# Two attention and mixture-of-experts layers on one core: the routing tables, the shared chunks and the opening of the second layer are rearranged

## The reference, cut to what matters

```python
x = x + L0_attention(layernorm(x), ctx)      # x: 16 sequences of 112 rows, 256 wide; 16 heads; ctx: 375 rows
x = x + L0_ffn(layernorm(x))
x = x + L1_attention(layernorm(x), ctx)
x = x + L1_ffn(layernorm(x))
# L0_ffn: each of the 1792 rows goes to 8 of 64 experts (inner width 128),
#   chosen by sigmoid scores in groups, and to one shared expert (inner width 256):
moe_out = einsum('tei,eih->th', silu(x @ Wg) * (x @ Wu) * coef, Wd)
shared  = silu(x @ SWg) * (x @ SWu) @ SWd
# L1_ffn: each row goes to 2 of 8 experts (inner width 704), no shared expert
```

## Time and profile before

| what | us |
|---|---|
| median of 3 runs | 1473.24 (1467.95 to 1477.11) |
| the profiled execution | 1479.25 |
| its span, first to last instruction | 1477.1 |
| PE busy in the span | 1242.9 (84%) |
| DVE busy | 879.1 (60%) |
| ACT busy | 500.2 (34%) |
| POOL busy | 434.9 (29%) |

### The profile page before, as it was taken

One profiled execution on the slowest core, in us unless ns is written; L12 is line 12 of the kernel. 1 busy time (PEld: TensorE's weight loads), 2 busy tenths in 40 slices (PEclk: granted clock), 3 DMA queues, 4 the chain that ended last, 5 costly groups with the idle time before them and its releaser, 6 DMA issues. The chain is left out here.

```text
span 1477.1 us, 40521 instructions
## 1 busy us (share of the span) xinstructions
PE 1242.9 (84%) x12614; PEld 955.0 (65%) x12615; DVE 879.1 (60%) x2766; ACT 500.2 (34%) x1240; POOL 434.9 (29%) x589
## 2 busy tenths in 40 slices
PE   5899999999877999996279998989996299999950
PEld 3566666665545999994146666656664299999950
DVE  2368788886676666662347767676764463444423
ACT  1355555453311444442035444444542011121110
POOL 0024554454341001000745555555221000000025
PEclk8799999998598999998569999998985699999985
DMA  7123434443224678857323433332213104223224
GB/s 190 53 75 110 113 110 111 110 108 88 83 60 147 191 220 263 239 167 241 95 74 87 100 80 94 78 93 75 72 38 128 28 23 157 99 89 118 77 64 120
DMA packets 118140, 164.96 MB, mean 112 GB/s; under 512 B 29426, under 2 KB 99026, under 8 KB 116932
## 3 DMA queue, kind: packets, MB, share of 16 engines
q0 software_dynamic: 19072, 67.13, 15.9%
q1 hardware_dynamic: 62036, 56.03, 14.0%
q10 hardware_dynamic: 36960, 40.93, 8.6%
HBM read 89.63 MB, written 58.21 MB: 100 GB/s over the span
## 5 line engine op out<-in xcount | busy, mean ns | idle before, releaser
L925 DVE TENSOR_REDUCE mx<-banks 112x2 f32<-112x750 f32 x256 | 235.1, 934 | 83.4 <-PE banks L584 81.2
L1616 POOL DMA_INDIRECT xs_d<-xns,idx x160 | 156.3, 977 | 193.6 <-PE banks L606 154.6
L1365 ACT ACTIVATE shared_buf<-banks 125x672 f32<-125x672 f32 x256 | 173.0, 728 | 75.5 <-PE banks L606 75.5
L799 PEld LDWEIGHTS banks<-xT,attn_buf 128*128 128x128 f32 x1408 | 163.8, 194 | 6.4 <-DVE xT L1221 4.5
L799 PE MATMUL banks<-xT,attn_buf 128*128 128x128 f32 x1408 | 164.7, 277 | 3.5 <-DVE xT L1221 3.5
L743 PE MATMUL banks<-xT,staged 128*128 128x128 f32 x1064 | 143.9, 279 | 6.6 <-DVE staged L1230 6.6
L1626 POOL DMA_INDIRECT kept<-y_d,yidx x128 | 125.7, 982 | 75.7 <-PE banks L606 35.2
L606 PE MATMUL banks<-attn_buf 18*125 18x112 f32 x3072 | 130.5, 303 | 14.9 <-DVE mx L925 14.0
L584 PE MATMUL banks<-attn_buf 17*112 17x375 f32 x1024 | 125.0, 560 | 13.5 <-DVE mx L925 12.7
L743 PEld LDWEIGHTS banks<-xT,staged 128*128 128x128 f32 x1064 | 131.3, 194 | 7.9 <-DVE xT L1221 7.2
L606 PEld LDWEIGHTS banks<-attn_buf 18*125 18x125 f32 x3072 | 106.3, 201 | 44.8 <-DVE mx L925 25.0
(11 more groups left out here) (191 smaller groups left out, 1789.1 us busy)
## 6 DMA issues: line engine op xcount, KB each, us to landing
shared_buf<-xs_d SPq DMA_DIRECT2D x172, 128.0 KB, 2.3
y_d<-shared_buf ACTq DMA_DIRECT2D x164, 128.0 KB, 2.5
ringbuf<-in_we POOLq DMA_DIRECT2D x8, 2176.0 KB, 9.6
ringbuf<-in_we POOLq DMA_DIRECT2D x32, 384.0 KB, 4.6
attn_buf<-attn_buf SPq DMA_DIRECT2D x128, 93.8 KB
attn_buf<-in_ctxT ACTq DMA_DIRECT2D x26, 375.0 KB
xs_d<-zrow ACTq DMA_DIRECT2D x16, 512.0 KB, 3.2
y_d<-zrow SPq DMA_DIRECT2D x6, 1024.0 KB, 9.2
```

The costliest lines, as they stand in the source:

```text
L799: last = pe.matmul(dst, staged[:, u % 2, k * 2 * L.I + c * P:k * 2 * L.I + (c + 1) * P], xT[:, u % 2, k, :], start=(k == 0), stop=(k == KD ...
L925: dve.tensor_reduce(mx[:, i % 2, 2 * p:2 * p + 2], banks[0:Q, 2 * p:2 * p + 2, 0:S], AX.X, ALU.max).then_inc(s_max, 1)
L1365: act.activation(pT[:, slot:slot + 2, :], banks[0:KT, first_bank:first_bank + 2, 0:ST * Q], ACT.Exp, scale=0.25).then_inc(s_exp, 1)
L1616: pool.indirect_dma_start(xs_d[L.number], bass.IndirectOffsetOnAxis(ap=idx[:, b % 2, k:k + 1], axis=0), xns[:, b % 4, :], None).then_inc(s ...
```

## The change

1. **Table rows by TensorE.** `tabc` becomes fp32. PE multiplies each of its ten columns with the identity, which puts 1 x 128 (or 1 x 64) numbers into banks 6 and 7. ACT copies tables 0 and 1 to `tabr`, DVE copies 2, 3 and 4. The two DMAs over DRAM go. `s_tabi` now counts these two copies.
2. **Order of `last()`.** The weights jobs (R4 or R3, W80, W81) of the last sequence come after the tables. SLOT comes before the weights job for the sequence before it. `(W81, -1)` moves into the wait for RK. POOL scatters the last six choices of sequence 13 before `deviation(1)` of 15.
3. **Shared chunks.** Chunks 0 and 1 are done in `last()`, woven into tables; chunks 2 and 3 come after `experts0`, at the start of the layer 1 opening. The kept copy of the transposed rows is split in two tensors.
4. **Skipped turns.** In layer 0 there is no Else branch. ACT writes the zeros for tiles 116 to 179 of `y_d` during attention of layer 0, four tiles in each of 16 DMAs. POOL waits at the end for the number of landed tiles worked out from the table.
5. **Tile loads.** The first four tiles are loaded without waiting for weights; DVE's `stage` waits for them.
6. **New opening of layer 1.** New FIRST_JOBS; POOL interleaves half gathers; DVE does chunks 2 and 3, the output rows of 4 to 15, and the bias and row maxima right after LN1 of b = 0.

```diff
-        FIRST_JOBS[1] = (("K0", 1), ("V2", 0), ("V01", 0), ("K1", 1), ("XT", 0), ("Q", 0), ("XT", 1), ("Q", 1)))
+        FIRST_JOBS[1] = (("XT", 0), ("Q", 0), ("V2", 0), ("V01", 0), ("K0", 1), ("K1", 1), ("BO", 0), ("ROWS", 0), ("MAX", 0), ("XT", 1), ("Q", 1)))
@@ SP tile_loads
-                for u in range(2):
-                    sp.wait_ge(s_scat[u], scat_count(l, B // 2))
-                sp.wait_ge(s_route, TABLES_READY[l])
-                sp.dma_start(tab_d[l].rearrange("k (c p) -> p k c", p=P), tabc[:, :, :], allow_slow_non_contiguous=True).then_inc(s_tabo, 16)
-                sp.wait_ge(s_tabo, 16 * (l + 1))
-                sp.dma_start(tabr[:, :, :], tab_d[l].rearrange("(o k) t -> o k t", o=1)).then_inc(s_tabi, 16)
-                sp.wait_ge(s_tabi, 16 * (l + 1))
+                sp.wait_ge(s_tabi, 2 * l + 2)
...
+                        if isinstance(first, int) and c == 0:
+                            for u in range(2):
+                                sp.wait_ge(s_scat[u], scat_count(l, B // 2))
+                            sp.wait_ge(s_zero, 16 * (2 * B + 1 if l == 0 else 2 * B + L.E + 2))
...
-            sp.wait_ge(s_dn[0], L0.tiles + 1)
             stream(L1)
@@ PE first, layer 1
-                        pe.wait_ge(s_ye[0], L0.tiles)
+                        free = [[(s_sev, B + SEV_CREDIT)], [(s_sev, B + SEV_CREDIT)]]
@@ PE last
                     job("RK", n, 1, [(ev["LG"], n + 1)])
+                    if l == 0:
+                        shared_down(0)
+                        shared_up(1)
+                    table_rows()
+                    if l == 0:
+                        shared_down(1)
+                def table_rows():
+                    pe.wait_ge(s_route, TABLES_READY[l])
...
+                    for r in range(5):
+                        for j in range(2):
+                            dst, col, width = (M0, (r * 2 + j) * P, P) if r < 2 else (M1, j * P, P) if r == 2 else (M1, 2 * P + (r - 3) * P + j * (P // 2), P // 2)
+                            last = pe.matmul(dst[0:1, col:col + width], tabc[:, r, j:j + 1], ident[:, 0:width], start=True, stop=True)
+                        if r in (1, 4):
+                            last.then_inc(s_tabm, 1)
@@ PE shared
+                pe.wait_ge(s_tiles, 1)
+                for i in range(2, 4):
+                    shared_up(i)
+                    shared_down(i)
@@ DVE
+                def first1():
+                    opening(SP_OPEN)
+                    shared_products(2)
+                    for b in range(3):
+                        for part in range(4):
+                            if (b, part) == (0, 2):
+                                shared_rows(2)
+                            extra(f"C{part}", base + b, b, b % 2)
+                            if b < 2:
+                                output_rows(L0, 4 * b + part + 4)
+                        extra("MOM", base + b, b, b % 2)
+                        if b == 0:
+                            shared_products(3)
+                        extra("LN1", base + b, b, b % 2)
+                        if b == 0:
+                            shared_rows(3)
+                            close()
+                            start(SP_OPEN + 1)
+                            bias()
+                            for i in range(2):
+                                for p in range(2):
+                                    row_max(base, i, p)
+                        if b == 1:
...
+                            for k in range(4):
+                                output_rows(L0, 12 + k)
@@ DVE last
+                    order = ([("W81", -2)] if l == 0 else []) + [("OT", 0)] + [(j, -1) for j in route_of[l:]] + [("OP", 0), ("RK", -1), ("LN2", 0)]
+                    order += [("SLOT", -1), (weights, -1), ("W80", -1)] + [(j, 0) for j in route_of] + [("W81", -1), ("RK", 0), ("SLOT", 0)]
                     for j, r in order:
                         extra(j, n + r, b + r if r <= 0 else 0, (r + 1) % 2)
+                    if l == 0:
+                        shared_products(0)
                     close()
+                    tables(L)
+                    table_in()
+                    if l == 0:
+                        shared_products(1)
+                    start(SP_LATE[l])
+                    if l == 0:
+                        shared_rows(0, (2, 3))
+                    for j in (weights, "W80", "W81"):
+                        extra(j, n, b, 1)
+                    if l == 0:
+                        shared_rows(1)
@@ DVE tables, after L1161
+                if l == 0:
+                    shared_rows(0, (0, 1))
@@ DVE experts0
-                    with dve.Else():
-                        dve.wait_ge(s_h[0], first + 1)
-                        dve.wait_ge(s_txe[0], first + 2)
-                        for done in (s_txe, s_stage, s_h):
-                            dve.sem_inc(done[0], L.unroll)
+                dve.memset(rinv[:, :], 0.0).then_inc(s_tiles, 1)
@@ ACT zero_rows
+                        act.dma_start(y_d[l][bass.ds((b * some + SURE) * P, some * P), :].rearrange("(t p) d -> p t d", p=P),
+                                      zrow[:, :].unsqueeze(1).to_broadcast([P, some, D])).then_inc(s_zero, 16)
@@ POOL first, layer 1
-                        gather(1, 1)
-                    for b in range(3):
-                        deviation(0, base + b)
-                        if l and b < 2:
-                            gather(b + 2, b)
+                        for b in range(3):
+                            gather(b + 1, (b + 1) % 2, 0, 4)
+                            deviation(0, base + b)
+                            gather(b + 1, (b + 1) % 2, 4, 4)
@@ POOL experts, layer 0
-                pool.wait_ge(s_yfill, 16 * sum(M.turns for M in LAYERS[:l + 1]))
+                    landed = pool.snap(((total + 3) >> 3) * 32 + 32)
+                    for done in s_yst[0] + s_xl[0]:
+                        pool.wait_ge(done, landed)
```

More of the change, by code:

```diff
@@ L458, in loads @@
                                 sp.wait_ge(s_txt[l], first + (c + u - EDGE + 1))
-                            load(u, rows[u], needs[u])
-                loads(0, 2 * EDGE, EDGE)
+                            if c >= weights_from:
+                                sp.wait_ge(s_wr[l], needs[u])
+                            load(u, rows[u])
+                loads(0, 2 * EDGE, EDGE, EDGE)
                 end = tiles_end(SP)
@@ L1050, in extra, with bias, opening @@
                         job(j, n, b, u)
-                def first():
-                    start(SP_ATTN[l])
+                def bias():
+                    dve.wait_ge(s_wts[l], REST_IN[l])
+                    dve.wait_ge(s_bo, l + 1)
+                    wait(dve, s_rb, l * B)
+                    link_signal(after().tensor_tensor(bo2[:, :], bank[7][0:Q, 0:D], bo[l][:, :], ALU.add), s_bo2, l + 1)
+                def opening(span):
+                    start(span)
                     c = C_R1 if l else C_R0
@@ L1521, in experts0 @@
                             body(first + u, u % 4)
-                    with act.Else():
-                        act.wait_ge(s_sil[0], first + 1)
-                        act.wait_ge(s_ye[0], first)
-                        for done in (s_sil, s_ye):
-                            act.sem_inc(done[0], L.unroll)
-                        stores_done(0, first)
-                for u in range(EDGE):
-                    act.wait_ge(s_xl[0][u], L.tiles * 4 + 16)
             def experts1():
@@ L1571, in _ @@
             attention(L0)
-            shared()
             experts0()
+            for i in range(2, 4):
+                shared_silu(i)
             attention(L1)
```

239 lines of the change are left out of this document (136 added, 103 removed).

## The result

The changed kernel takes 1435.24 us (median of four, 1430.99 to 1443.29) beside 1474.78 of the kernel before (four, 1467.95 to 1477.11): ratio 0.974, 95% interval 0.972 to 0.977, which is 34 to 42 us less. The forecast was 1441. Ratios leave out executions in the chip's slower state: in all that follows that is one, the longest of the six of `e1_tables_dram`. The profiled execution took 1435.35, with a span of 1433.7; the span before was 1477.1.

A forecast was written before the change was run, and what follows sets the result against it. TensorE's idle time was placed in three passages between the big stages. 25.2 + 0 + 7.7 - 1 = 31.9 us off the profiled 1479.25 gave 1447.3; that execution lay 6.0 above the median, so 1441, range 1426 to 1456.

The forecast's parts named there:

- Layer 0 tables, 25.2: Passage before layer 0's experts: first gate matmul at 439.7 instead of 464.9, gain 25.2 us, bounds 17 to 27.
- DVE's list behind it: Layer 0 tables: DVE's work from `tabr` ready to the first gate matmul, taken as 11.7 us.
- The margin of the weights: Layer 0 tables: weights reported 1.5 us before the first four tiles need them, from about 439.
- rival 1: Layer 0 tables: the weights set the start of `experts0`; POOL's reports 6 us late give 1447; chance 0.10.
- Opening, 0: Opening of layer 1: POOL's 14.8 us won are lost again in DVE's list; gain 0, bounds 5.5 either way.
- XT of sequence 0: Opening of layer 1: this TensorE step starts at about 710.5, against 721.2 in the old trace.
- deviation(0, 1): Opening of layer 1: POOL stands here from about 715 until DVE has sequence 1's moments at 739.
- DVE leaving the loop: Start of the layer 1 opening: six skipped turns without Else work take 3.5 us, bounds 2 and 6.2.
- XT to BO: Opening of layer 1: TensorE's steps counted at 10.1 us full clock, 15.8 half; 12 taken.
- Rival 2: Opening of layer 1: the gathers set its end; gain 15, total 1426; chance 0.14.
- Layer 1 tables, 7.7: Passage before layer 1's experts: first gate matmul at 1162.2 against 1169.89, gain 7.7 us, bounds 6 and 9.
- Zero writes, 1: Layer 0 attention: ACT's one more 512 KB write per body costs 1 us in all, bounds 0 and 51.

The follow-up runs named there:

- e1_tables_dram: Masked kernel (e0) with the tables again going over DRAM by two SP DMAs; first gate matmul 23.8 and 16.6 us after the tables, against 15.0 and 9.9.
- e3: Masked kernel (e0) with output rows of sequences 8 to 15 moved into DVE's bodies 0 and 1 of layer 1; total 6.7 us longer than e7.
- e7: Masked kernel (e0) with three 512 KB zero writes per layer 0 attention body instead of one; up to 0.5 us further behind than the changed kernel at sequence 14.
- e8: e5_both with output rows put where DVE waits in the opening, only row 15 in body 0; ratio to the kernel before 0.961, opening 53.4 us.
- e9: e8 with TensorE's bias product ahead of sequence 1's keys, row 12 before the bias sum, rows 13 to 15 in body 0; 1413.0 us, ratio 0.958.
- e5_both: Masked kernel (e0) with the DVE order of e4_second_first and output rows 8 to 15 in bodies 0 and 1; 1418.4 us, opening 53.5.
- e0: The masked kernel: changed kernel with the weights-wait register masked with 127 and one SP semaphore count added; ratio to the kernel before 0.976.
- e10: Masked kernel (e0) with the last sequence's weights jobs, W80 and W81 ahead of the tables again; ratio to the kernel before 0.975.
- e2_zero_last: Masked kernel (e0) with unused y_d tiles zeroed by SP in the skipped turns, as before; opening 84.5 us against 74.5, medians 7.1 apart.
- e6_shared_all_first: Masked kernel (e0) with all four shared chunks before layer 0's experts; 21 us later at the tables, opening 7 to 11 less, total 9.2 more than e7.
- e4_second_first: Masked kernel (e0) with sequence 1's combine, output rows, moments and LN1 ahead of DVE's bias sum; opening 59.1 us against 74.5, medians 15.6 apart.

## Why the prediction was right, step by step

The mechanism was right passage by passage: DVE's list decides at the layer 0 tables, the gathers don't decide the opening, and the trip goes. The size was 7.6 us short (31.9 of 39.5), most of it in stages and clocks for which the sum had no term.

- **Layer 0 tables, 25.2.** On the clock of the trace 24.8. From the last normalisation it is 71.8 to 48.1, 23.7, in e3, e7, e8, e9 25.0 to 26.0 and in `e5_both` 27.2: right. That the sum meets the middle of these is in part luck: the level of TensorE's clock in `shared_down(0)`, up to 3 us, wasn't in it. Inside, two errors work against each other: `tabr` was ready at 429.25, 2.3 later than worked out on the clock of before (attention ended 1.1 earlier), since TensorE's matmuls stand behind `shared_up(1)`, which the prediction had in mind only as what keeps the clock up (in `e5_both`, with `shared_down(0)` at 3.71 us, they start 0.1 behind the tables), and DVE's list behind it took 10.9 instead of 11.7. The margin of the weights was 0.3 us, not 1.5: rival 1 was closer than its 0.10, and `e1_tables_dram` shows it deciding as soon as the tables are later.
- **Opening, 0.** Of the five executions with this opening, the two with `shared_down(3)` at 3.71 us gained 3.0 and 2.8 (changed, `e1_tables_dram`), and the three in which TensorE's clock made it 6.5 to 6.7 lost 0.5 to 1.2 (e0, e7, e10). The forecast lies between them, without having had this term. The chain was as written: XT of sequence 0 worked out at 710.5 and, on the clock of before (27.94 later), at 710.05; deviation(0, 1) at 739 and at 736.2; DVE's wait at the bias sum about 10 and 10.45; POOL's over 15 and 19.62. Terms that were off: DVE leaving the loop 4.26, not 3.5; XT to BO 10.25, not 12. Rival 2 (the gathers set it) is refuted by POOL's waits; But the 0 is a sum of two larger terms: POOL's earlier start is worth 10 us in the new opening (`e2_zero_last`), not nothing, and the shared chunks moved there cost it 7 to 11 (`e6_shared_all_first`).
- **Layer 1 tables, 7.7.** 39.5 to 30.8 from the last normalisation, 8.7. The matmuls took 3.37, not 4.0, and tabr to gate 5.44, not 5.7. The split in the prediction (2.05 for the moved job and W81, the rest for the trip) doesn't hold: put back alone, the jobs cost 0.4 to 0.8 (e10) and the trip 6.6 (e1), and both 8.7 to 9.5, since each covers part of the other.
- **Zero writes, 1.** 0.3, up to the last body but one.
- **Not in the sum:** `experts0` is 3 us shorter (215.1 and 216.6 before, 211.5 to 213.7 in all twelve others), of which the lower clock behind the first gate matmul (to 471.35 before, to 444.03 after: 6.5 and 3.9 us of it) accounts for 1.3 and the rest is open; and attention of layer 1 is 2 to 6 shorter, in part by TensorE's clock (above).
- **The two profiled executions** are 43.4 apart, 11.5 more than 31.9: `experts0` 3.2, the opening 3.0, attention and tables of layer 1 4.9 (12.6 for 7.7), the first passage 0.6 (24.8 for 25.2 - 1), less 0.2 at the end. The medians are 39.5 apart, since the profiled execution of the kernel before lies 4.5 above its median and the other one doesn't.
- **Not undone alone:** the earlier tile loads (edit 5), the order of POOL's scatters (in edit 2) and the new FIRST_JOBS and half gathers (edit 6). What each brings isn't shown.

## What to carry to other kernels

Where an engine has spare time behind a wait, ask which of its later work another engine is waiting for: here one move in DVE's order (`e4_second_first`, 11.5 to 15.6 us) was worth about as much as the whole table trip. Freeing an engine that isn't the last to arrive buys only what its first consumer had to wait for it (POOL 17.2 us earlier bought 10), so look at the same time at the order of the engine that it waits for. Fit small jobs by where their engine waits, stage by stage: four rows of 1.1 us cost body 1 of layer 1 about 2 us and nothing where DVE waits in the opening, though the totals don't show the difference. And before a difference between two profiles is put down to an edit, compare TensorE's clock in the stretch: here it moved single stages by 3 to 8 us.

## What the runs showed of the hardware

- Leaving a loop over six skipped turns with nothing in them takes DVE 4.26 us (changed kernel, 651.66 to 655.92), an estimate of 0.7 us a turn with the loop's exit in it. TensorE's 4.59 us there end with DVE's signal, so its own price isn't shown.
- Writing the table of 5 KB to DRAM, one number per run of memory, took 10.6 and 10.0 us (before) and 11.5 and 9.5 (`e1_tables_dram`) until the next DMA was issued; reading it back, 1.6 to 3.0 until an engine went on.
- Three writes of 512 KB in each body of attention, beside its small DMAs, 24 MB in all, cost 0.8 us up to the last body but one of layer 0, 341 us from the start.
- The same 16 records of TensorE in `shared_down` took 3.71 us at a granted clock of 1.00 and 6.5 to 6.7 at 0.53 to 0.54; the 20 records of the table rows 1.92 us at 1.00 (layer 0) and 3.37 at 0.55 (layer 1).
- The same kernel took 1534 us on one chip and 1475 to 1477 on the others. The profile of the masked kernel there has a granted clock of 0.894 (0.906 in `e7_zero_three` on another chip), attention of layer 1 424.8 (392.8) and from the first gate matmul of layer 1 to the end 313.4 us (306.5).
